# Matmuls that nobody reads in TensorE's waits at the ends and beginnings of blocks

## The reference

```
x = _rmsnorm(latents, s1)
latents = latents + _attn(x, inputs, wq_c, wk_c, wv_c, wo_c, rep)
y = _rmsnorm(latents, s2)
latents = latents + _swiglu_ffn(y, w1_1, w2_1)
z = _rmsnorm(latents, s3)
latents = latents + _attn(z, z, wq_s, wk_s, wv_s, wo_s, rep)
t = _rmsnorm(latents, s4)
latents = latents + _swiglu_ffn(t, w1_2, w2_2)
```

## Time and profile before

| | us |
|---|---|
| median of 3 runs | 2048.26 |
| lowest and highest | 2045.43 and 2050.31 |
| the profiled execution, its own time | 2057.58 |
| its span, first to last instruction | 2055.8 |
| PE busy | 1776.4 (86%) |
| DVE busy | 1332.9 (65%) |
| ACT busy | 866.2 (42%) |
| POOL busy | 629.1 (31%) |
| mean granted clock of TensorE | 0.932 |

### The profile page before, as it was taken

One profiled execution on the slowest core, in us unless ns is written; L12 is line 12 of the kernel. 1 busy time (PEld: TensorE's weight loads), 2 busy tenths in 40 slices (PEclk: granted clock), 3 DMA queues, 4 the chain that ended last, 5 costly groups with the idle time before them and its releaser, 6 DMA issues.

```text
span 2055.8 us, 34270 instructions
## 1 busy us (share of the span) xinstructions
PE 1776.4 (86%) x10630; PEld 1237.2 (60%) x10630; DVE 1332.9 (65%) x3354; ACT 866.2 (42%) x2513; POOL 629.1 (31%) x732
## 2 busy tenths in 40 slices
PE   5969999769996878988779999896888979898988
PEld 4746665558985656655565555483444845455567
DVE  5866767301117876788666676796677966556665
ACT  3735554322334643565324444342332435444521
POOL 2325555210022234676320000130000325455534
PEclk9979998879998978999789999997998989999999
DMA  4100000468862000002100010101000100000200
GB/s 167 37 20 15 13 7 16 147 217 301 307 236 82 0 1 31 32 30 71 67 8 16 16 69 0 42 11 62 0 0 19 55 1 12 23 11 11 72 1 18
DMA packets 36627, 115.15 MB, mean 56 GB/s; under 512 B 2961, under 2 KB 23345, under 8 KB 29345
## 3 DMA queue, kind: packets, MB, share of 16 engines
q1 hardware_dynamic: 33968, 107.33, 15.2%
q0 software_dynamic: 2544, 6.43, 1.0%
HBM read 99.34 MB, written 14.40 MB: 55 GB/s over the span
## 4 chain that ended last, share of the span: by engine, by line
PE 44%; issue 20%; DVE 14%; POOL 14%; ACT 4%; DMA 3%; SPq 1%; POOLq 0%; DVEq 0%; ACTq 0%
POOL arena L2020 11%; PE ps L1008 7%; PE ps L1048 4%; PE ps L821 4%; PE ps L873 3%; PE ps L1168 3%; PE ps L1152 3%; PE ps L927 3%; PE ps L816 3%; PE ps L947 2%; PE ps L891 1%; PE ps L863 1%; DMA wml<-in_wm_L_moe 1%; PE ps L933 1%; ACT arena L1286 1%
## 5 line engine op out<-in xcount | busy, mean ns | idle before, releaser
L2020 POOL TENSOR_TENSOR arena<-arena,rinv 112x375 f32<-112x375 f32 (+1 forms) x448 | 371.1, 830 | 489.9 <-DVE rinv L1675 479.7
L891 PEld LDWEIGHTS ps<-cst,arena 112*125 112x125 f32 (+1 forms) x1408 | 188.1, 184 | 176.6 <-POOL arena L2020 88.9
L891 PE MATMUL ps<-cst,arena 112*125 112x112 f32 (+1 forms) x1408 | 247.0, 294 | 45.2 <-POOL arena L2020 39.9
L1286 ACT ACTIVATE arena<-ps,negmax 112x375 f32<-112x375 f32 (+1 forms) x384 | 190.6, 501 | 168.2 <-DVE negmax L1670 167.8
L1684 DVE COPY arena<-ps 125x336 f32<-125x336 f32 x384 | 190.8, 497 | 47.3 <-PE ps L891 44.9
L2073 POOL TENSOR_TENSOR w_split_sb<-wml,w_split_sb 128x512 fp32r<-128x512 f32 (+1 forms) x40 | 45.9, 1148 | 527.0 <-ACT w_split_sb L1352 525.1
L1670 DVE TENSOR_REDUCE negmax<-ps 112x1 f32<-112x375 f32 (+1 forms) x288 | 158.3, 550 | 70.9 <-PE ps L863 61.9
L1008 PE MATMUL ps<-h_split_sb,w_split_sb 128*128 128x448 f32 x768 | 179.7, 383 | 17.8 <-DVE h_split_sb L1559 7.1
L1286 ACT ACTIVATE arena<-arena,negmax 112x112 f32<-112x112 f32 (+1 forms) x256 | 125.4, 491 | 139.1 <-DVE negmax L1659 97.0
L1008 PEld LDWEIGHTS ps<-h_split_sb,w_split_sb 128*128 128x128 f32 x768 | 150.4, 198 | 35.9 <-DVE h_split_sb L1559 13.2
L816 PE MATMUL ps<-wat,arena 128*125 128x256 f32 (+1 forms) x608 | 153.5, 390 | 16.8 <-DVE arena L1600 9.5
(11 more groups left out here) (221 smaller groups left out, 3186.7 us busy)
## 6 DMA issues: line engine op xcount, KB each, us to landing
wml<-in_wm_L_moe SPq DMA_DIRECT2D x21, 1028.0 KB, 7.7
wml<-in_wm_L_moe SPq DMA_DIRECT2D x21, 1024.0 KB, 7.7
craw<-in_ctx SPq DMA_DIRECT2D x40, 375.0 KB
wml<-in_wm_L_m SPq DMA_DIRECT2D x3, 3072.0 KB, 13.8
wat<-in_wa_L_ca SPq DMA_DIRECT2D x2, 2560.0 KB, 10.2
wml<-in_wm_L_m SPq DMA_DIRECT2D x2, 2048.0 KB, 10.1
keys_hbm<-arena SPq DMA_DIRECT2D x8, 375.0 KB
values_hbm<-vz SPq DMA_DIRECT2D x8, 375.0 KB
```

The source lines that it names most:

```text
L891: last = nc.tensor.transpose(ps[0:blk.kp, T_BANK + s % blk.t_banks, o:o + S], buf[:, i * blk.nk + q * blk.kp:i * blk.nk + (q + 1) * blk.kp ...
L1286: last = go(probs[0:S, s % blk.nprobs, i * nk:(i + 1) * nk], src[:, i * nk:(i + 1) * nk], ACT.Exp, scale=-1.0 if blk.mask == "input" else ...
L2020: pool.tensor_tensor(p3, p3, r3, ALU.mult).then_inc(scaled, 1)
```

## The change

A helper `keep_busy(bank, times)` issues `times` matmuls of the 128 x 128 identity by itself into a PSUM bank. Nothing waits for them, and what they write is overwritten before anyone reads the bank. A table `WARM` names the blocks and the places. They all stand on TensorE's program, outside the hardware loops:

- `tail={s: k}`: k matmuls in step s of `body(B)`, ahead of the step's `turn` or `weigh`.
- `tokens=k`: ahead of the first `turn_tokens` for the MLP.
- `first=k`: ahead of `up(0)`. `second=k`: between the transposes of the fourth pair and `up(2)`.
- `out=k`: at b = 6 of the final transposes, ahead of the wait for bank 0.
- `scores=k`: ahead of the first scores of the block.
- `QT0=k`: ahead of the wait for the normed queries of batch 0.

The table has 19 entries with 214 matmuls. The other engines' programs and all waits are as before, but for a wait for `out_done` in front of the QT0 fill, which has been reached by then.

```diff
+WARM = {
+    "L1_sa": dict(tail={1: 7}, tokens=5),
+    "L1_m1": dict(second=8, out=12),
+    "L1_ca": dict(scores=14, tail={3: 9}),
+    "L1_m2": dict(first=6, second=8, out=12),
+    "L2_ca": dict(QT0=20, tail={1: 22}),
+    "L2_m1": dict(second=9, out=12),
+    "L2_sa": dict(QT0=24, tail={0: 10}),
+    "L2_m2": dict(second=9, out=12),
+    "L3_ca": dict(tail={3: 6}),
+    "L3_m": dict(second=9),
 }
...
         def _(pe):
+            def keep_busy(bank, times):
+                for _ in range(times):
+                    nc.tensor.matmul(ps[:, bank, 0:P], ident, ident, start=True, stop=True)
+
             def attention(n):
                 blk, st = BLOCKS[n], START[n]
+                warm = WARM.get(blk.name, {})
+                spare = 7 if blk.out_bank != 7 else blk.w_banks[1]
...
                         if i == 0:
+                            if isinstance(m, int) and m == 0 and "QT0" in warm:
+                                pe.wait_ge(out_done, st["out"])
+                                keep_busy(O_BANK, warm["QT0"])
                             pe.wait_ge(qk_ready, count(st["qk"], 1, m, 1))
...
+                if "scores" in warm:
+                    keep_busy(O_BANK, warm["scores"])
+
                 def body(b):
                     for s in steps(b, blk, blk.out_step + 1):
+                        if b == B and s in warm.get("tail", {}):
+                            keep_busy(spare, warm["tail"][s])
...
                             pe.wait_ge(exped, START[n + 1]["unit"])
+                            keep_busy(spare, warm.get("tokens", 0))
                             for b2_ in range(SOON):
                                 turn_tokens(n + 1, b2_)
...
+                warm = WARM.get(blk.name, {})
+                keep_busy(5, warm.get("first", 0))
                 for t in range(2 * FC + 2):
                     if t == 2:
                         for b2_ in range(SOON, B // 2):
                             turn_tokens(n, b2_)
+                        keep_busy(5, warm.get("second", 0))
...
+                    if b == 6:
+                        keep_busy(5, warm.get("out", 0))
                     if OUT_BANKS.index(OUT_BANKS[b]) < b:
                         pe.wait_ge(out_done, st["out"] + OUT_BANKS.index(OUT_BANKS[b]) + 1)
```

More of the change, by code:

```diff
@@ L88 @@
         out_step=5, lag=4, s_banks=3, t_banks=2, w_banks=[7, 3], out_bank=7),
+}
+WARM = {
[9 more added lines that the diff above has]
+    "L3_m": dict(second=9),
 }
```

## The result

The changed kernel takes 2031.93 us (2031.04 to 2033.13, 4 runs) against 2049.28 (2045.43 to 2052.42, 4 runs) of the kernel before beside it: 0.9917, 95% interval 0.9898 to 0.9935. By these medians 17 to 20 us come back. The forecast was 28 us and 2020 us; the time lies in its range of 2008 to 2040. One single run of all that follow, 2444.77 us at a granted clock of 0.683, is of a slow state that no other run here shows, and the medians and ratios leave it out.

A forecast was written before the change was run, and what follows sets the result against it. TensorE was taken as the chain's largest part (44%), slowed by half clock behind waits. Eight terms sum to 29.9 us, less 2; 28 off the profiled 2057.6 us, itself 9.3 above the median, gave 2020 us, range 2008 to 2040.

The forecast's parts named there:

- nothing changes: Rival: identity matmuls do not count as work for the clock, falls stay, fills hidden; 2044 to 2052 us, chance 0.05.
- it gets slower: Rival: falls stay and fills run at half clock, overrunning by about 15 us; 2063 us, chance 0.05.
- all of TensorE's time comes back: Rival: 38 to 58 us back, 1990 to 2010 us, chance 0.07.
- Term 1: `out` of L1_m1, with the last transposes and the Q piece of L1_ca: 1.2 us back.
- Term 2: `scores` of L1_ca: the wait for keys by DMA stays 3.85 us, TensorE's work behind it speeds up; 5.0 us back.
- Terms 3 and 4: `out` of L1_m2, 3.1 us back; `out` of L2_m1 and L2_m2, 5.8 us back together.
- one fall at a new place: Deduction of 2 us from the sum, because a sooner TensorE waits longer elsewhere.
- Term 5: `QT0` of L2_ca and L2_sa: transposes and first scores behind the wait, 1.8 and 3.0 us back, 4.8 together.
- Term 6: `second` in the three gated MLPs, full clock when TensorE arrives: 0.9, 1.7 and 1.7 us, 4.3 together.
- Term 7: L1_sa with L1_m1, L1_ca with L1_m2: a fall remains behind the first twelve matmuls but ends sooner; 3.0 us back.
- Term 8: `tail` in L2_ca, L2_sa and L3_ca: 1.0 us, nothing and 1.7 us back, 2.7 together.
- the part-way rival: Fills hold the clock only in part, since waits stay partly open: 4 to 18 us, 2030 to 2044 us, chance 0.21.

The follow-up runs named there:

- The divided fill: Changed kernel with L1_ca's 14 scores matmuls split, 9 ahead of the wait for X's last updates and 5 behind: 2027.26 us, 1.3 us below the changed kernel.

## Why the prediction was right, and where it was off

**Right: the direction, the mechanism, the price.** Identity matmuls hold the clock, most fills end before their waits or close to it, and right behind them the same instructions run at the full-clock durations of the earlier trace rows. The changed kernel's rows behind the second and third `out` fill:

```profile
1044.11 2.85 PE L835 MATMUL ps<-wat,arena 128*125 128x256 f32 x12
...
1384.14 3.66 PE L840 MATMUL ps<-wat,arena 128*112 128x512 f32 x8 [0.78 <-ACT arena L1257]
```

2.85 for 4.88 us and 3.66 for 6.17. Sixteen matmuls of 128 x 128 gave a price of 0.225 us; `out`, 12 of them, takes 2.84 us with its tail. Of the rivals, that nothing changes, that it gets slower and that all of TensorE's time comes back did not happen. Of the signs that I named, the eight L840 take 3.66 and 3.69 us as forecast, but the clock is not 1.00 across 806 to 830 us nor through the first batches of L2_ca and L2_sa, and its mean is 0.958, not 0.965.

**Off: the size.** I set the two profiled traces against each other, each of TensorE's 10630 instructions with its twin, and read the lead right before and behind each term. The lead is 3.5 us before the first fill, which the change can't have made, and 25.7 at the end: 22 us, of 29.9 in the sum. The medians say 17 to 20. What the remaining 3 to 5 us are stays open; the kernel before alone differs by as much from run to run. The steps that failed are terms 2, 5 and 6, each by what it left out of the path; term 7 was mis-sized the other way.

- Term 1 (`out` of L1_m1): 1.1 us, forecast 1.2.
- **Term 2 (`scores`): 2.9 us, forecast 5.0. This step failed in how I read the program.** I took the whole wait of 3.85 us to be open to the fill. The fill stands behind a wait for the last updates of X, which VectorE reaches 2.07 us later (row 805.06 above). The clock fell at 806.3 us under the fill, it took 5.02 us in place of 3.15, and TensorE itself became what the scores waited for (the fill's L779 is 17.0% of the chain that ended last over 806 to 830 us): 2.9 us of lead were lost, 5.8 gained behind it. The divided fill shows the first half of this by 2.1 us sooner.
- Terms 3 and 4 (`out` before L2_ca, L2_sa, L3_ca): 2.9, 3.0 and 2.0 us, forecast 3.1 and 5.8 for the last two. Then came a new fall at 1645.9 us, in L3_ca's KP pieces, behind waits of 0.94, 0.78 and 0.90 us between the pieces (0.78, 0.37 and 0.76 before). It took 1.7 us of lead, and the wait for VectorE behind it gave them back, 0.48 us where it had been 2.12:

```profile
1678.15 0.83 PE L835 MATMUL ps<-cst,arena 125*128 125x125 f32 x6 [2.12 <-DVE arena L1643]
...
1645.60 7.10 PE L835 MATMUL ps<-wat,arena 128*125 128x256 f32 x24 [0.90 <-ACT arena L1263]
...
1654.27 0.83 PE L857 MATMUL ps<-cst,arena 125*128 125x125 f32 x6 [0.48 <-DVE arena L1676]
```

  (The first line is of the kernel before, the others of the changed one.) So the "one fall at a new place" came, and the 2 us taken off for it were not lost here.
- **Term 5 (`QT0`): 0.8 us lost in the first batch of L2_ca and 0.6 gained in that of L2_sa, forecast 4.8. This is the largest step that failed.** The fill held the clock and the eight transposes behind it were fast. What I missed is what the changed kernel's rows show next:

```profile
1060.49 0.54 PE L857 MATMUL ps<-cst,arena 125*128 125x125 f32 x3 [0.87 <-ACT arena L1297]
1061.54 0.54 PE L857 MATMUL ps<-cst,arena 125*128 125x125 f32 x3 [0.51 <-ACT arena L1297]
1062.86 1.83 PE L895 MATMUL ps<-arena 128*125 128x448 f32 x2 [0.78 <-ACT arena L1301]
...
1402.00 6.13 PE L840 MATMUL ps<-wat,arena 128*112 128x512 f32 x8 [0.84 <-ACT arena L1257]
```

  Short pieces at full clock, each with a wait for ScalarE's copy ahead, and at 1062.3 us the clock is down; likewise in L2_sa at 1400, in front of the eight L840. I had put the waits into the sum as time that doesn't shrink, and not as what takes the clock down. Fills in them bring the clock to 1.00 there and, by the traces, 5.5 us more through the two first batches, before a further fall took 2.5 back. The warning was in the trace of the kernel before. I wrote that every fall follows waits of 1.88 to 6.83 us; that was misread, for the fall at 986.9 us, one of my seventeen, has only these and shorter waits in the 10 us ahead of it:

```profile
984.88 0.55 PE L891 MATMUL ps<-cst,arena 112*125 112x112 f32 x3 [0.61 <-DVE arena L1684]
986.45 0.55 PE L891 MATMUL ps<-cst,arena 112*125 112x112 f32 x3 [1.01 <-DVE arena L1684]
```

  Over the rest of L2_sa the changed kernel's first profile gains another 0.5 us, and the two repeats of the same kernel 4 to 5 us, since of the kernel before's two half-clock stretches in its loop only one came in them; no term had these in it.
- **Term 6 (`second` in the gated MLPs): 2.5 us, forecast 4.3**, by block 0.4, 0.6 and 1.5 where I had 0.9, 1.7 and 1.7. TensorE is faster there, but then waits for VectorE's split: ahead of the first L1076 of L2_m1 1.01 us (row below) where it had been 0.19.

```profile
1323.96 1.50 PE L1076 MATMUL ps<-g_split_sb,w_split_sb 128*128 128x448 f32 x6 [1.01 <-DVE g_split_sb L1859]
```

- **Term 7 (L1): 5.4 us, forecast 3.0, and not in the way that I said.** The fall that I put behind the first twelve L1036 came in neither MLP of this profile; in L1_m1 the clock fell sooner, at 744.8 us, and was back for the fill. It was up for the twelve L1036 of L1_m2 and stayed up over a wait that had grown to 2.88 us, as forecast, but without harm:

```profile
995.76 0.60 PE L1022 MATMUL ps<-cst,arena 112*128 112x112 f32 x4 [2.88 <-DVE arena L1546]
```

  In the two repeats of the same kernel the same wait, 2.84 us, was followed by a short fall (1000.7 and 998.3 us). A place near the edge is decided from one execution to the next.
- Term 8 (`tail`): 1.6, 0 and 0.4 us, forecast 1.0, 0 and 1.7. In L2_ca twelve L927 stood in the stretch (4.14 us, now 2.48), not six; in L3_ca the fill ran at half clock, and in the two repeats, where it did not, the gain was 0.6 us.

With 0.5 us over the rest of L2_sa these add up to the 22 us.

**The profiled execution.** I took 28 us off 2057.6 and 9.3 more as if the whole were an offset. It was near the upper end of a spread of 2041 to 2062 us, and before the first fill, where no kernel here differs from another, the other profiles are 0.1 to 6.6 us ahead of it. A sum over one execution's half-clock stretches holds for that execution, and the gain in the median was smaller.

The case that came true lies at the border of two of mine: the forecast's 18 to 38 us and the part-way rival's 4 to 18. The measured 2031.93 us is outside the forecast's own 2010 to 2030 and inside the rival's 2030 to 2044. The rival's reason is the right one, and I had given it 0.21; the stated range held because it took in most of that rival.

## What to carry to other kernels

Filling a long wait keeps the clock up over it; look at what TensorE does next. Where that is dense work, as behind the `out` fills, the fill is worth what the half clock had cost there (48 matmuls, 10 us). Where it is short pieces with a wait of 0.5 to 1.4 us ahead of each, fill these too, or the clock falls a few us later and the long fill brings little (0 to 4 us for 44 matmuls). A fill behind an earlier wait starts late: look for the first wait that TensorE stands at (dividing the one fill that did brought 1.3 us, which is inside the spread). Make a fill a little shorter than the wait at full clock, since both half and double the length cost (8.6 and 20.9 us); a piece that becomes faster makes the next wait longer, so look at the timeline again after each round. One profile shows one draw of where the clock falls; take the gain from repeated runs.

## What the runs showed of the hardware

- Float32 matmuls and float32 transposes of an identity hold the granted clock alike: 1.00 over and behind the `out` fills, where it was 0.50 without (806.0, 1055.3 and 1400 us).
- Waits of 0.5 to 1.4 us in a row between short pieces were followed by half clock (1062 and 1400 us) in five profiles of five, also behind a QT0 fill of twice the length, and in none of three where they were filled. One wait of 2.88 us behind dense work was not followed by it (995.76 us); the same wait of 2.84 us in two repeats was.
- The same program takes 2041 to 2062 us from run to run, the longer the lower its mean granted clock (0.940 at 2044.37, 0.931 at 2058.31 us), and its half-clock stretches come out at slightly other places; what places them was not found.
